# Layer 1 of a two-layer gated cross-attention block: halves made in SBUF and turned by DMA transposes instead of TensorE transposes

## The reference

```python
x = x + jnp.tanh(g_xattn[1]) * _L1_xattn_ref(_layernorm(x), ctx_1024, ctx_1024, Wq, Wk, Wv, Wo)   # 16 heads, depth 64
x = x + jnp.tanh(g_ffn[1]) * _L1_ffn_ref(_layernorm(x), prototypes, B, A, bias, temp)

# _L1_ffn_ref: 32 prototypes, rank 16, the two nearest prototypes of each row are used
w = softmax(-dists / t); topw, topi = top_k(w, 2); topw = topw / sum(topw)
for tslot in range(2):
    h = einsum('nri,ni->nr', B[topi[:, tslot]], xf)
    out = out + topw[:, tslot:tslot+1] * (einsum('nor,nr->no', A[topi[:, tslot]], h) + bias[topi[:, tslot]])
```

## Time and profile before

| | us |
|---|---|
| median of 3 runs (3070.83 to 3072.63) | 3070.93 |
| profiled execution | 3073.06 |
| its span | 3071.0 |
| layer 1's even part, one body of two tiles | 24.57 |

### The profile page before, as it was taken

How to read it: one execution, slowest core, us unless ns; L and a number is a source line. 1 busy time by engine, 2 the same in 40 slices (tenths; PEclk the granted TensorE clock), 3 DMA queues, 4 the chain that set the end, 5 groups by cost and what they waited for, 6 DMA issues and landing times.

```text
span 3071.0 us, 98317 instructions
## 1 busy us (share of the span) xinstructions
PE 2849.6 (93%) x32554; PEld 2275.0 (74%) x32554; DVE 2558.1 (83%) x6445; ACT 1830.5 (60%) x3605; POOL 2154.9 (70%) x3859
## 2 busy tenths in 40 slices
PE   4889896899999999689899999999999999999997
PEld 2444444677777778567688888888888888888886
DVE  6787786788888888665899999998989899999986
ACT  2666765677787777575455555555555555555553
POOL 3893000666666766554598888888888888888887
PEclk9999998899999999899999999999999999999999
DMA  5997666233332323631544444444434444444441
GB/s 153 351 343 293 238 245 258 68 91 83 80 93 79 93 76 95 226 101 36 127 105 106 109 101 99 95 96 103 104 87 107 96 99 99 94 96 104 105 89 43
DMA packets 367618, 388.75 MB, mean 127 GB/s; under 512 B 118432, under 2 KB 341264, under 8 KB 362320
## 3 DMA queue, kind: packets, MB, share of 16 engines
q1 hardware_dynamic: 346960, 335.42, 39.8%
q0 software_dynamic: 7328, 23.40, 2.5%
q10 hardware_dynamic: 12960, 25.23, 2.2%
HBM read 235.08 MB, written 148.83 MB: 125 GB/s over the span
## 4 chain that ended last, share of the span: by engine, by line
PE 39%; DVE 6%; issue 3%; POOL 2%; ACT 2%; DVEq 0%; POOLq 0%; ACTq 0%
PE banks L150 11%; PE banks L152 11%; PE banks L151 11%; PE banks L1306 2%; PE banks L1291 2%; DVE a_probT_lo L1393 1%; PE banks L1338 1%; DVE a_pick L1518 1%; ACT a_qT_hi L1195 1%; DVE a_y L1537 1%; DVE a_rsum L1405 1%; PE banks L1361 1%; DVE a_wsel L1527 0%; PE banks L1353 0%; ACT a_ynT_hi L1195 0%
## 5 line engine op out<-in xcount | busy, mean ns | idle before, releaser
L1195 ACT ACTIVATE a_qT_hi<-banks 128x512 f16<-128x512 f32 x252 | 150.5, 597 | 700.6 <-PE banks L152 700.6
L383 POOL TENSOR_TENSOR a_probT_lo<-a_expT,a_probT_hi 128x512 f16<-128x512 f32 x256 | 291.5, 1160 | 218.3 <-ACT a_probT_hi L466 218.3
L459 ACT ACTIVATE a_expT<-banks,a_top,w_score_scale 128x512 f32<-128x512 f32 (+1 forms) x384 | 272.6, 710 | 152.1 <-PE banks L550 145.9
L1108 POOL TENSOR_TENSOR a_pn<-a_prob,a_rsum 128x1024 f32<-128x1024 f32 (+1 forms) x256 | 307.3, 1222 | 5.1 <-DVE a_rsum L1407 5.0
L150 PE MATMUL banks<-a_xnT_hi,w_q_hi 128*128 128x256 f16 x1024 | 281.3, 275 | 4.7 <-DVE a_xnT_lo L1391 3.0
L150 PE MATMUL banks<-a_vo_front,a_probT_hi 128*128 128x256 f16 x1024 | 279.0, 272 | 2.7 <-DVE a_probT_lo L1393 2.6
L152 PE MATMUL banks<-a_xnT_hi,w_q_lo 128*128 128x256 f16 x1024 | 280.7, 274 | 0.0
L151 PE MATMUL banks<-a_xnT_lo,w_q_hi 128*128 128x256 f16 x1024 | 280.5, 274 | 0.0
L152 PE MATMUL banks<-a_vo_front,a_probT_lo 128*128 128x256 f16 x1024 | 279.1, 273 | 0.0
L151 PE MATMUL banks<-a_vo_front,a_probT_hi 128*128 128x256 f16 x1024 | 279.0, 272 | 0.0
L1393 DVE SCALAR_TENSOR_TENSOR a_probT_lo<-banks,a_probT_hi 128x512 f16<-128x512 f32 (+1 forms) x384 | 212.5, 582 | 34.4 <-ACT a_probT_hi L1195 34.0
(11 more groups left out here) (383 smaller groups left out, 10363.1 us busy)
## 6 DMA issues: line engine op xcount, KB each, us to landing
vo<-kv_vo_out SPq DMA_DIRECT2D x38, 2048.0 KB, 7.9
a_vo_front<-vo SPq DMA_DIRECT2D x128, 512.0 KB
kt<-kv_k_out ACTq DMA_DIRECT2D x9, 2560.0 KB, 14.9
a_k<-kt SPq DMA_DIRECT2D x64, 308.0 KB, 3.5
kv_raw_e<-in_L_ffn_w POOLq DMA_DIRECT2D x16, 1024.0 KB, 9.4
a_x<-in_x SPq DMA_DIRECT2D x64, 256.0 KB, 2.9
a_y<-in_x SPq DMA_DIRECT2D x64, 256.0 KB, 2.8
x<-a_y SPq DMA_DIRECT2D x64, 256.0 KB, 2.9
```

The costliest lines, as they stand in the source:

```text
L383: pool.tensor_tensor(probT[b][1][:, first:end, :], expT[b][:, first:end, :], probT[b][0][:, first:end, :], ALU.subtract).then_inc(prob_rea ...
L459: act.activation(expT[1 - h][0:rows, first:end, :], bank, ACT.Exp, bias=top[0:rows, 0:1], scale=weights["score_scale"][0:rows, 0:1]).then_ ...
L1108: last = pool.tensor_tensor(keys_of(pn[h]), keys_of(prob_of(u, h, 2)), rsum[h][:, :].unsqueeze(2).broadcast_to([P, H, n]), ALU.mult)
L1195: act.activation(out, bank[:, 0:cols].rearrange("p (c s) -> p c s", c=out.shape[1]), ACT.Copy, scale=scale)\
```

## The change

For three activations the order of turning and splitting is reversed. The halves are made from the f32 tile in SBUF, side by side in one f16 tile, and one DMA transpose turns both.

| | before | after |
|---|---|---|
| rows `xn`, once a body | 4 TensorE transposes to a bank, two halves `xnT` from it | `xn_parts` (128 x 1024 f16), DMA transpose to `xnT[p]` |
| second norm `yn`, once a tile | 2 transposes, halves `ynT` | `yn_parts` (128 x 512), DMA transpose to `ynT[p]` |
| `hw`, once a tile | 4 transposes, halves `hwT` | `hw_parts` (128 x 1024), DMA transpose to `hwT[p]` |

The up product moves from tile t-7 to t-8 and stands right after the scores (`LAG` 8). The bank ring has 20 uses a body. SP issues the transposes behind waits; the one of `hw` stands behind the one of `yn`, and both stand ahead of the tile's store. VectorE makes the low half of `hw` between maximum and shift, that of `yn` after the shift, and that of the rows at the end of a body. The eight loads of `vo_back` become one; for it the last 13 keys of `pn` are stored key by key.

```diff
-    LAG = 7
+    LAG = 8
@@ sync
-            for n in range(MAIN):
-                sp.dma_start(vo_back[p][n * BACK:(n + 1) * BACK, :, :, :], values_back(batch_at(i), n)).then_inc(vo_in[p], 16)
+            sp.dma_start(vo_back[p][:, :, :, :], values_back(batch_at(i))).then_inc(vo_in[p], 16)
+        def turn_rows(i, u, j):
+            p, _ = turn(u, j, 2)
+            begin(xn_lo, i)
+            begin(q_ready, (i - 1) * QU)
+            sp.dma_start_transpose(xnT[p][:, :, :], xn_parts[:, :, :, :].rearrange("p a s d -> p (a s d)")).then_inc(xnT_in[p], 16)
+        def turn_normed(t, p):
+            begin(yn_lo, t + 1)
+            begin(low_ready, (t - 1) * LU)
+            sp.dma_start_transpose(ynT[p][:, :, :], flat(yn_parts[:, :, :])).then_inc(ynT_in[p], 16)
+        def turn_weighed(t, p):
+            begin(hw_lo, t + 1)
+            begin(out_ready, t - 1)
+            sp.dma_start_transpose(hwT[p][:, :, :], flat(hw_parts[:, :, :])).then_inc(hwT_in[p], 16)
...
@@ gpsimd, normalise
-            for keys_of, n in ((first_keys, FRONT), (last_keys, BACK)):
-                last = pool.tensor_tensor(keys_of(pn[h]), keys_of(prob_of(u, h, 2)),
-                                          rsum[h][:, :].unsqueeze(2).broadcast_to([P, H, n]), ALU.mult)
...
+            pool.tensor_tensor(last_by_key(pn[h]), last_keys(e).rearrange("p (n a) k -> p a k n", a=2),
+                               rsum[h][:, :].rearrange("p (n a) -> p a n", a=2).unsqueeze(2)
+                               .broadcast_to([P, 2, BACK, MAIN]), ALU.mult).then_inc(pn_ready, 1)
@@ scalar
+        def normed_high(t, u, h, j):
+            need(act, yn_ready, t + 1)
+            if live(t - 1, NT):
+                earlier, times = turned_place(5, u, h, j)
+                need(act, ynT_in[earlier], (times + 1) * 16)
+            act.activation(yn_parts[:, 0, :], yn[:, :], ACT.Copy).then_inc(yn_hi, 1)
...
@@ tensor
+                if live(t - 8, NT):
+                    turned, times = turned_place(8, u, h, j)
+                    need(pe, hwT_in[turned], (times + 1) * 16)
+                    need(pe, wselT_ready, t - 7)
+                    bank = bank_for(i, ("ffn", h))
...
@@ vector
+        def rows_low(i):
+            need(dve, xn_hi, i)
+            nc.vector.tensor_tensor(xn_parts[:, :, 1, :], xn[:, :, :], xn_parts[:, :, 0, :], ALU.subtract).then_inc(xn_lo, 1)
+        def normed_low(t):
+            need(dve, yn_hi, t + 1)
+            nc.vector.tensor_tensor(yn_parts[:, 1, :], yn[:, :], yn_parts[:, 0, :], ALU.subtract).then_inc(yn_lo, 1)
+        def weighed_low(t):
+            need(dve, hw_hi, t + 1)
+            nc.vector.tensor_tensor(hw_parts[:, 1, :], hw[:, :], hw_parts[:, 0, :], ALU.subtract).then_inc(hw_lo, 1)
```

More of the change, by code:

```diff
@@ L939, in attention_ffn_phase @@
     yn = sb("yn", [P, D])
-    ynT = pair("ynT", [P, DC, P])
+    yn_parts = sb("yn_parts", [P, 2, D], F16)
+    ynT = [sb(f"ynT{p}", [P, 2 * DC, P], F16) for p in range(2)]
     ysq = sb("ysq", [P, TPB])
@@ L950, in attention_ffn_phase @@
     hw = sb("hw", [P, LOW])
-    hwT = pair("hwT", [P, LC, P])
+    hw_parts = sb("hw_parts", [P, 2, LOW], F16)
+    hwT = [sb(f"hwT{p}", [P, 2 * LC, P], F16) for p in range(2)]
     first_x = [sb(f"first_x{n}", [P, D]) for n in range(FIRST_X)]
@@ L1332, in body @@
                         scores(i, t, h, u, j)
[L1333 to L1336 removed]
+                if live(t - 8, NT):
[3 more added lines that the diff above has]
+                    bank = bank_for(i, ("ffn", h))
                     for c in range(LC):
[L1338 to L1339 removed]
+                        matmul3(nc, bank[:, 0:D], [hwT[turned][:, s * LC + c, :] for s in range(2)],
+                                [w[:, c, :] for w in ffn["up"]], c == 0, False)
+                    filled(nc.tensor.matmul(bank[:, 0:D], wselT[:, :], ffn["bias"][:, :], start=False, stop=True),
+                           i, ("ffn", h))
                 if live(t - 5, NT):
[L1342 removed]
+                    turned, times = turned_place(5, u, h, j)
+                    need(pe, ynT_in[turned], (times + 1) * 16)
                     for n in range(LU):
@@ L1346, in body @@
                         for c in range(DC):
-                            last = matmul3(nc, bank[:, 0:cols], [a[:, c, :] for a in ynT],
+                            last = matmul3(nc, bank[:, 0:cols], [ynT[turned][:, s * DC + c, :] for s in range(2)],
                                            [w[:, c, n, 0:cols] for w in ffn["down"]], c == 0, c == DC - 1)
@@ L1493, in body @@
                 if live(t - 7, NT):
-                    split_lo(i, ("hwT", h), hwT[0][:, :, :], hwT[1][:, :, :], LC * P, hwT_hi, t - 6, hwT_ready)
+                    weighed_low(t - 7)
                 if live(t, NT):
                     shift_scores(t, h, u)
+                if live(t - 4, NT):
+                    normed_low(t - 4)
+                if live(t - 8, NT):
+                    bank = full(i, ("ffn", h))
+                    y8 = y_sb[slot(8)]
+                    nc.vector.scalar_tensor_tensor(out=y8[:, :], in0=bank[:, 0:D], scalar=ffn["scale"][:, 0:1],
+                                                   in1=y8[:, :], op0=ALU.mult, op1=ALU.add).then_inc(out_ready, 1)
                 if live(t - 5, NT):
@@ L1533, in body @@
                     nearest_index(t - 5)
-                if live(t - 7, NT):
-                    bank = full(i, ("ffn", h))
-                    y7 = y_sb[slot(7)]
-                    nc.vector.scalar_tensor_tensor(out=y7[:, :], in0=bank[:, 0:D], scalar=ffn["scale"][:, 0:1],
-                                                   in1=y7[:, :], op0=ALU.mult, op1=ALU.add).then_inc(out_ready, 1)
+                if h == 1 and live(i + 2, NB):
+                    rows_low(i + 2)
                 prep(3)
```

171 lines of the change are left out of this document (84 added, 87 removed).

## The result

The changed kernel takes 3297.12 us (median of 4, 3285.42 to 3306.24) where the kernel before takes 3071.78 (3070.83 to 3075.17) beside it: a ratio of 1.0731, with a 95% interval of 1.0714 to 1.0749. The profiled execution took 3292.56 us for a span of 3290.8. The forecast was 3113 with a range of 3005 to 3225, so the sign was right and the size was wrong by more than a factor of five: +225 us, not +42.

A forecast was written before the change was run, and what follows sets the result against it. TensorE bound the kernel, GpSimd close behind; GpSimd at 23.4 + 1.7 + 0.1 = 25.2 us a body would then bind: 60 x 0.63 = +38, plus 4 at the end, 3113 us. Range 3005 to 3225, the forecast's own 3095 to 3125.

The forecast's parts named there:

- Three engines close together: Loop body of 24.57 us: TensorE works 24.3 us, GpSimd needs 23.4, VectorE 23.1, all within 1.5 us.
- the collision: VectorE's five new two-SBUF-input low halves a body delay GpSimd's steps: GpSimd loses 1.7 us a body.
- about 0.8 of short waits: VectorE's addition to its 23.1 us a body, leaving it below GpSimd's 25.2 us.
- five of 25 uses of the banks go with them: Bank uses that disappear with the removed TensorE transposes; no cost was put on this.
- The 16 transposes: f32 transposes of `xn`, `hw`, `yn` leave TensorE: 1.76 us a body, 24.3 down to 22.5.
- VectorE held: Rival: the shared port costs VectorE, its low half of `hw` waiting for `pn`; 26.4 us a body, 3185 us; chance 0.14.
- gaps found: Rival: GpSimd's small steps take most collisions, 1.7 us falls to 0.1; body 23.5 us, time 3011 us; chance 0.24.
- Normalise: GpSimd's second part, written key by key: 0.05 us more a tile, 0.1 a body, bounds 0 and 0.3.
- the rival with L = 12 us: DMA transpose ring binds; L runs from low half to landing; body 29.7 us, about 3380 us; chance 0.15.
- the ring: Waits through DMA transposes of `hw`: two issues of 0.4 us, landing 3.5, L 4.3; hidden, binding from L = 6.9 us.
- could only gain: Dropping seven of eight `vo_back` loads frees SP, off the path; costed at nothing.
- No wait of GpSimd for `mv`: Sign of a right forecast: GpSimd no longer waits for VectorE's mean and variance, 1.1 us a body before.

The follow-up runs named there:

- e11: e6 with the five low halves made from one SBUF input (copies, output not the reference's): 3058 us, ratio 0.9960.
- e9: Kernel before plus one idle VectorE operation a tile with one SBUF input, ahead of the low half of `hw`: 3109 us, ratio 1.0116.
- e1: Changed kernel with VectorE's scaled up product moved ahead of the low half of `hw`: 3258 us, ratio 1.0590.
- e2: Changed kernel with the low halves made from one SBUF input (copies, output not the reference's): 3120 us, ratio 1.0145.
- e6: Changed kernel with the low halves of `yn` and `hw` ahead of the maximum, shift behind the scaled product; two inputs kept: 3169 us, ratio 1.0307.
- e3: Changed kernel with the edits of e1 and e2 together (output not the reference's): 3095 us, ratio 1.0064.
- e4: Kernel before with only the last keys' new layout: one load of `vo_back`, second part of `normalise` key by key: 3076 us, ratio 1.0004.
- e7: e6 with the last keys' old layout (eight loads, old second part of `normalise`): 3144 us, ratio 1.0236.
- e5: e3 with the last keys' old layout (eight loads, old second part of `normalise`; output not the reference's): 3182 us, ratio 1.0349.

## Why the prediction was wrong

**What bounds the kernel.** Three engines close together was right. For GpSimd I had 23.4 us; e11, where it paces, says 24.20 - 0.56 = 23.6. For VectorE I had 23.1; e9 with 1.33 us more lasts 25.20. If VectorE paces there, which was not tried, what hangs on it needs 23.9 and its room is 0.7 us, half of the 1.5 that I read from the earlier trace rows: its waits for ScalarE's halves are not all room.

**Which steps failed.** Two. The larger is in the collision: GpSimd was to lose 1.7 us a body, and VectorE was to "stay below" with "about 0.8 of short waits". VectorE lost 2.2 us itself. The other is "five of 25 uses of the banks go with them", costed at nothing. Neither gives the time by its own length: with both, VectorE's lost time lies in front of a bank that TensorE waits for. The next paragraphs take them in the order of the prediction.

**What is removed.** The 16 transposes were priced at 1.76 us; 24.3 to 22.9 is 1.4. The five uses of the banks were not free. A ring with fewer uses pairs other uses: the bank of `q` now hangs on the scaled product, 3.1 us of TensorE's wait a body (154.3 us in 1400 / 28.01 = 50 bodies), and the low clock level behind it. By e1 that is 39 us of the 225, though the waits that e1 uncovers hide part of its worth.

**The collision.** The mechanism was the right one, and so was the size of GpSimd's share: 1.7 us forecast, 1.6 measured (24.0 us of busy time a body, 22.3 in e2). It is made up otherwise than I had it: 2 x (1128 - 822) ns on the second part, 2 x (1206 - 1059) on `hw`, and 0.7 us in its other steps. What failed is who pays. I let one engine pay, with a rival in which the other pays (`VectorE held`, 3185). In the changed kernel both pay: VectorE 2 x (1174 - 664) + 2 x (855 - 418) + (993 - 667) ns = 2.2 us a body. And what VectorE loses ahead of the scaled product lengthens TensorE's wait for the bank (93.7 us without it in e2, 154.3 with it), which the forecast had no link for. By e2 the collision is 177 us of the 225; in my sum it was 1.7 x 60 = 102. Where GpSimd alone pays, in e6, the 1.86 us come near the 1.7 partly by luck: a tile costs it 0.88 us where my prices give 0.63, and the four small steps alone make 1.76, so that little is left for the low half of the rows (0.45 in my sum).

**What is left.** The two causes overlap: 39 and 177 alone, 202 together (e3). That leaves 3095, where my sum without a collision has 3011 (`gaps found`). Of these 84 us, 37 go when the transposes are issued earlier (e11, 3058). Of the other 47, `normalise` is 0.46 x 60 = 28 and GpSimd's 23.6 for 23.4 is 12.

**Normalise.** 0.05 us a tile was taken from the nearest plain form, with bounds of 0 and 0.3 a body. It is 0.28 a tile, 0.56 a body, outside my bounds. The new inner run, with stride and a changing second operand, had no row of before. It cost nothing in e4; where GpSimd paces, the old layout with its eight loads is 24 us faster (e6 and e7).

**The transposes through DMA.** The landing was right (3.2 us for 3.5), so the rival with L = 12 us did not come. The sentence with 1309 ns a block in the Trainium skill ("VectorE: DVE Perf Modes", section "The three transpose paths") would have made eight blocks in sequence an estimated 10.5 us; the trace has 3.2 from issue to landing for eight, so they don't go one after another at that price. The issue was mis-sized: 1.2 to 2.5 us on SP where I took 0.4, hence an L of 5.1 us in the median in e3 and not 4.3. And the ring binds earlier than the 6.9 that I had worked out: TensorE waits for more than half of the up products. In e3 that, with GpSimd's 24.2, holds the body at 24.63; that it is these two together is argued from e11 and e5, not tried alone. And the loads of `vo_back`, which "could only gain", were worth 87 us in the queue of the transposes.

**The signs in the profile.** A longer body, TensorE's waits and stretched steps of GpSimd were named and came; TensorE is busy for 85% and not 90. "No wait of GpSimd for `mv`" did not: it waits 106.6 us, 62.6 before in the same stretch, so it is not the pace. The low half of `hw` at 1.5 us or more beside `pn`, the sign of the rival, came in 39 of 100 tiles.

**The clock.** It is a small part of the 39 us of e1. Between 1600 and 3000 us the granted clock is 0.50 for 105.8 us in the changed kernel, 2.1 us a body, and for 99.0 us in e1, 1.9 a body. In the former 22 of the 29 low stretches follow a wait for the bank, in e1 12 of the 22 a wait for `hwT`. At half the clock half of such time is lost, so the two differ by about 0.1 us a body, 6 us in 60. In e2, whose waits for the bank are shorter (longest 1.8 us), the clock is low for 3.4 us in all.

What stays open: it was not tried what sets the 28.01 us, since every engine waits for another there. No complete kernel here beats the one before; e11 shows that the idea would give 13 us if a low half could be made without a second SBUF input.

## What to carry to other kernels

Before you move a split from PSUM to SBUF, count the SBUF inputs of each VectorE operation: in these runs a second one and a GpSimd operation excluded each other for the whole operation, and with both engines nearly full another place in the order only moved the price to the other one. When the list of uses of a ring changes, write down for every use which earlier use has its bank now, and who reads that one last. An edit that frees a queue is to be costed together with the edit that fills it.

## What the runs showed of the hardware

- A VectorE subtraction f32 minus f16, 128x512, takes 0.66 to 0.69 us with one SBUF input, or with two where it meets nothing; beside GpSimd's operation of 1.9 us it took 1.90 in the meeting shown and 2.29 at most. A GpSimd step of one column (0.19 us) took 0.56 beside such an operation. The later one waits until the other is through.
- SP needs 1.2 us in the median to issue a DMA transpose of 128 or 256 KB, now and then 2 us or more (2.5 in e3's row), against 0.4 for a plain load of rows; eight small loads of 26 KB need 7.9 us (e5), one of 208 KB 0.44. The landing of eight 128x128 blocks in f16 takes 3.2 us.
- GpSimd's product over 208 columns takes 0.82 us for 0.54 when its inner run is strided and its second operand changes along it; the two were not tried apart.
- After 2.07 us without work TensorE's granted clock stayed at 1.00 for another 0.4 us and then was 0.50 (1.2 GHz) for 3.2 us, with work queued all the while. In e2, with such waits of up to 1.8 us, it was 0.50 once in 1400 us.
